# Bias product as a 129th column, chunk rows written by ScalarE, own banks for the last row: a two-layer graph network on one core

## The chip, the cores and the metric

One core of one Trainium2 chip runs the whole kernel. The metric is the device time of one execution in microseconds (us). Five engines work side by side, each in its own program order, and meet only at semaphores: TensorE (PE in the profile), VectorE (DVE), ScalarE (ACT), GpSimd (POOL) and SyncE (SP, which here only issues transfers).

## The reference

Inputs are `x` (4096 x 128), a sparse row-normalised `adj` (4096 x 4096), and small weights. Cut to what matters:

```python
h = relu(layernorm(x))
# first layer: hyperbolic graph layer
g    = h_add(exp0(log0(h) @ embed), embed_bias)
neigh= exp0(adj @ log0(g))
out  = exp0(log0(concat(h, neigh)) @ layer)      # layer = (256 x 128)
x    = x + h_add(out, layer_bias)
h = relu(layernorm(x))
# two attention layers, each:
s = beta * (h/|h|) @ (h/|h|).T ; s = where(adj > 0, s, -1e9)
h = leaky(softmax(s) @ h)                        # slope 0.3
x = x + h
```

Here `exp0(v) = tanh(|v|) v/|v|`, `log0(y) = atanh(|y|) y/|y|`, and `h_add(a, y)` is a weighted sum of `a` and `y` whose two weights need `a.a`, `y.y` and the product `a.y` of each row with the bias `y`.

## The kernel before

Rows are cut in 8 chunks of 512 (4 blocks of 128). Four stages follow one another.

**Opening.** VectorE computes the layer norm, `log0` and the first `h_add`, TensorE the `embed` product and the product of `h` with the upper half of `layer` (`h1_sb`), ScalarE copies them out of PSUM.

**Chunks.** `aggregate` on TensorE multiplies the adjacency tiles of chunk c (loaded by SP in a ring) with all rows: 32 fp32 matmuls of 512 columns. ScalarE copies the result (`at_sb`); after the first tile of the next chunk TensorE runs `layer_product`: four transposes (`rows_ps`) and four matmuls with the lower half of `layer` (`w_ps`). ScalarE takes the squared lengths of the rows (`row_lengths`, L802), and then VectorE runs the chain of the chunk (`gnn_chunk`), a row of dependent instructions on 4 or 8 values per partition (`norm`, `inv_sqrt`, `atanh_over`, `product_scalars`, about 0.2 us each) with passes over 512 columns between them: `t1 = w * scale + h1` (L1283), its squares (L1288), its product with the bias `lb` (L1293), `t2 = lb * weight` (L1305), `t1 = t1 * weight + t2` (L1308), `t1 += x` (L1311), statistics, deviations, `t2` = the normalised rows after relu (L1331), their high and low fp16 halves in `src[0]` (L1334, L1336), and `t3`, the rows of unit length (L1342). ScalarE gives tanh and ln on request (`ask` / `answered`; the counter `asked` goes up on VectorE, `told` on ScalarE), and copies `t1` back to `x_sb`. TensorE transposes `t3` one chunk later (L456, before tile 4 of the chunk after next), ScalarE and VectorE leave it in halves in `xt[0]` (`split_columns`).

**The last chunk beside the first attention slots.** The attention layers work on 72 pairs of chunks (a, b >= a) each in two halves, 144 half-pairs in all, one per slot n of an order written out by hand: scores (`pair_scores`, L622), exp on ScalarE into `values` (`raise_scores`, L990), high halves (`high_halves`, L1000), low halves on VectorE (`low_halves`, L1647), eight transposes for the mirrored block (`turns`, L608), the mask by the adjacency (`own_mask` L1655, `mirrored_mask` L1665), and the weighted sums (`own_sum`, `mirrored_sum`). Slots 0 to 13 don't need chunk 7. So the last chunk's chain (`last_chunk` on VectorE and on ScalarE) is cut in 13 pieces, and `pause(i)` puts slot i + 1 between them. `chunk_norms` comes after pause 2, `chunk_deviations` before pause 9.

**Rows.** Each chunk row a gathers its sums in `own_ps` (two PSUM banks), the mirrored part in `mirror_sums`. At the end of a row VectorE adds both in `sums_in` and inverts the denominators (`row_total`), ScalarE scales (`row_averages`, L1020), VectorE applies leaky and, in the second layer, adds to `x_sb` (`row_leaky`, L1690, L1694). GpSimd stores the chunk (L403). The next row's `own_sum` waits until `own_ps` has been read (`total_made`).

## Time and profile before

| | |
|---|---|
| times of 3 runs | 981.88, 978.26, 982.6 us; median 981.88 |
| profiled execution | 978.14 us, its span 976.6 us, granted TensorE clock 0.989 |
| TensorE matmul busy | 929.2 us, 95% of the span |
| VectorE busy | 818.8 us, 84% |
| ScalarE busy | 511.2 us, 52% |
| GpSimd busy | 8.0 us |
| transfers | 207.26 MB, mean 212 GB/s |

The span runs from the first to the last instruction of one profiled execution; its device time is 1.5 us longer. Busy time of matmuls is modelled, since they are pipelined, so that a share near 100% says that TensorE has no gap, not that it is at its peak. The aggregation runs from about 57 to 291 us, the first attention layer until about 620 us, the rest is the second.

### The profile page before, as it was taken

How to read it: one execution, taken by the hardware profiler on the slowest of the kernel's cores; microseconds unless marked ns; L12 is line 12 of the kernel's file. 1: busy time of each engine (PE TensorE's matmuls, PEld its weight loads, DVE VectorE, ACT ScalarE, POOL GpSimd, SP SyncE). 2: the span in 40 equal slices, each digit the busy share in tenths (PEclk: the TensorE clock that was granted, in tenths of full speed). 3: DMA queues.
4: the chain of work that ended last, by engine and by line, in shares of the span. 5: the costliest groups of instructions: out<-in, count | busy, mean ns of one | idle time of the engine just before them, and what ended most of it. 6: DMA issues, size and time to landing. Idle time of an engine off the chain costs nothing.

```text
span 976.6 us, 22955 instructions
## 1 busy us (share of the span) xinstructions
PE 929.2 (95%) x9012; PEld 695.3 (71%) x9012; DVE 818.8 (84%) x2110; ACT 511.2 (52%) x756; POOL 8.0 (1%) x21
## 2 busy tenths in 40 slices
PE   2989999999996999999999999999999999999996
PEld 2944444444444878888888888778888888888885
DVE  7891888888889987888989898998778887888887
ACT  1711122212126685766656667787565565656564
POOL 0000000000000000000000000000000000000000
PEclk9899999999998999999999999999999999999999
DMA  8338988888861445565465555545565655665630
GB/s 301 143 118 285 307 285 287 277 295 283 301 229 44 174 173 207 196 246 212 179 235 192 222 217 193 180 167 217 197 217 198 246 197 204 221 232 189 246 142 36
DMA packets 29971, 207.26 MB, mean 212 GB/s; under 512 B 3632, under 2 KB 4272, under 8 KB 5296
## 3 DMA queue, kind: packets, MB, share of 16 engines
q1 hardware_dynamic: 28224, 203.44, 57.6%
q0 software_dynamic: 640, 2.10, 0.5%
q8 instruction: 71, 1.16, 0.5%
q10 hardware_dynamic: 1008, 0.33, 0.1%
q14 instruction: 28, 0.23, 0.1%
HBM read 203.75 MB, written 2.10 MB: 211 GB/s over the span
## 4 chain that ended last, share of the span: by engine, by line
PE 69%; DVE 22%; issue 5%; ACT 3%; DMA 1%; DVEq 0%; POOL 0%; SPq 0%; POOLq 0%
PE s_ps L622 17%; PE s_ps L608 10%; PE acc_ps L469 6%; PE acc_ps L675 6%; PE acc_ps L671 6%; PE acc_ps L673 6%; PE acc_ps L652 5%; PE acc_ps L648 5%; PE acc_ps L650 5%; DVE small L1132 1%; DVE small L1134 1%; DVE small L1133 1%; DVE work L1647 1%; ACT work L990 1%; PE s_ps L427 1%
## 5 line engine op out<-in xcount | busy, mean ns | idle before, releaser
L990 ACT ACTIVATE work<-s_ps,beta_bias,beta_scale 128x1024 f32<-128x1024 f32 x144 | 173.4, 1204 | 217.0 <-PE s_ps L622 216.9
L469 PE MATMUL acc_ps<-ring,set 128*128 128x512 f32 x512 | 223.8, 596 | 3.2 <-DVE set L1245 3.2
L1665 DVE SCALAR_TENSOR_TENSOR h_all<-ring,s_ps 128x1024 f32<-128x1024 f32 x112 | 136.7, 1221 | 65.5 <-PE s_ps L608 64.3
L469 PEld LDWEIGHTS acc_ps<-ring,set 128*128 128x128 f32 x512 | 96.8, 191 | 120.3 <-issue 117.6
L1647 DVE TENSOR_TENSOR work<-work 128x1024 f16<-128x1024 f32 x96 | 132.5, 1380 | 5.4 <-ACT work L1000 5.4
L1000 ACT ACTIVATE work<-work 128x1024 f16<-128x1024 f32 x96 | 131.5, 1369 | 3.2 <-DVE work L1655 0.2
L1655 DVE SCALAR_TENSOR_TENSOR work<-ring,work 128x1024 f32<-128x1024 f32 x96 | 116.8, 1217 | 0.0
L622 PE MATMUL s_ps<-xt 128*128 128x512 f16 x432 | 106.4, 382 | 3.8 <-ACT work L990 3.0
L622 PE MATMUL s_ps<-set 128*128 128x512 f16 x432 | 105.0, 379 | 0.5 <-ACT work L990 0.5
L671 PE MATMUL acc_ps<-set,work 128*128 128x129 f16 x576 | 102.4, 219 | 2.7 <-DVE accs L1682 2.7
L671 PE MATMUL acc_ps<-src,work 128*128 128x129 f16 x576 | 103.5, 220 | 1.4 <-DVE work L1655 1.4
L675 PE MATMUL acc_ps<-src,work 128*128 128x129 f16 x576 | 103.9, 224 | 0.0
L673 PE MATMUL acc_ps<-src,work 128*128 128x128 f16 x576 | 103.6, 221 | 0.0
L675 PE MATMUL acc_ps<-set,work 128*128 128x129 f16 x576 | 102.7, 222 | 0.0
L673 PE MATMUL acc_ps<-set,work 128*128 128x128 f16 x576 | 102.5, 219 | 0.0
L652 PE MATMUL acc_ps<-set,h_all 128*128 128x129 f16 x448 | 79.8, 222 | 0.0
L652 PE MATMUL acc_ps<-src,h_all 128*128 128x129 f16 x448 | 79.8, 222 | 0.0
L650 PE MATMUL acc_ps<-src,h_all 128*128 128x128 f16 x448 | 79.6, 219 | 0.0
L650 PE MATMUL acc_ps<-set,h_all 128*128 128x128 f16 x448 | 79.6, 219 | 0.0
L648 PE MATMUL acc_ps<-src,h_all 128*128 128x129 f16 x448 | 79.6, 219 | 0.0
L648 PE MATMUL acc_ps<-set,h_all 128*128 128x129 f16 x448 | 79.6, 219 | 0.0
L608 PE MATMUL s_ps<-ident,work 128*128 128x128 f32 x560 | 73.6, 274 | 3.0 <-DVE work L1647 3.0
(260 smaller groups left out, 1723.2 us busy)
## 6 DMA issues: line engine op xcount, KB each, us to landing
ring<-in_adj_t SPq DMA_DIRECT2D x192, 1024.0 KB, 5.0
x_sb<-in_x SPq DMA_DIRECT2D x4, 512.0 KB, 7.2
out<-x_sb POOLq DMA_DIRECT2D x8, 256.0 KB, 2.8
w<-in_layer ACTq DMA_DIRECT2D x2, 64.0 KB, 8.1
w<-in_embed ACTq DMA_DIRECT2D x1, 64.0 KB, 4.2
eb<-in_embed_bias ACTq DMA_DIRECT2D x1, 64.0 KB, 6.9
lb<-in_layer_bias ACTq DMA_DIRECT2D x1, 64.0 KB, 7.9
beta<-in_beta ACTq DMA_DIRECT2D x2, 0.5 KB, 7.2
```

Source lines behind the costliest of these rows:

```text
L469: last = nc.tensor.matmul(agg, v_sb[:, jb, :], ring[:, k, b, :], start=jb == 0, stop=jb == NB - 1)
L608: ins = nc.tensor.transpose(turn_ps[:, ib, ts(u, P)], words[x.n % WR][:, ds(u * CH + ib * P, P)], ident[:, :])
L622: last = nc.tensor.matmul(score_ps[:, ts(u, CH)], xt[x.la][:, p, ds(x.b * CH + (x.h * HB + u) * P, P)], xt[x.la][:, q, ds(x.a * CH, CH)], ...
L648: nc.tensor.matmul(mir_ps[:, x.h, o], w[:, WORD_HI, col], src[x.la][:, q, F:AW], start=ib == 0, stop=False)
L650: nc.tensor.matmul(mir_ps[:, x.h, ds(u * PW, F)], w[:, WORD_HI, col], src[x.la][:, q, 0:F], start=False, stop=False)
L652: last = nc.tensor.matmul(mir_ps[:, x.h, o], w[:, WORD_LO, col], src[x.la][:, q, F:AW], start=False, stop=ib == CB - 1)
L671: nc.tensor.matmul(own_ps[:, ib // 2, ds(ib % 2 * PW, PW)], w[:, WORD_HI, col], src[x.la][:, q, F:AW], start=opens, stop=False, skip_group ...
L673: nc.tensor.matmul(own_ps[:, ib // 2, ds(ib % 2 * PW, F)], w[:, WORD_HI, col], src[x.la][:, q, 0:F], start=False, stop=False, skip_group_c ...
L675: last = nc.tensor.matmul(own_ps[:, ib // 2, ds(ib % 2 * PW, PW)], w[:, WORD_LO, col], src[x.la][:, q, F:AW], start=False, stop=False, ski ...
L990: nc.scalar.activation(values[x.n % VR], score_ps, ACT.Exp, bias=beta_bias[:, x.la:x.la + 1], scale=beta_scale[:, x.la:x.la + 1]).then_inc ...
L1647: V.tensor_tensor(w[:, WORD_LO, :], values[x.n % VR], w[:, WORD_HI, :], ALU.subtract)\
L1665: V.scalar_tensor_tensor(turned[x.off % MR].rearrange("p (b j) -> p b j", b=CB), ring[:, x.mir_tile % AR, :, ds(x.h * HB * P, HB * P)], 0. ...
```

## The change

The bias product becomes a 129th column of the two products with `layer`: a column `layer @ layer_bias` is appended to `w1` and `w2` (two more VectorE instructions in the opening, for which the first of these products now waits), so `w_ps` and `h1_sb` carry 129 columns, and `t1 . lb` is `bias_column * scale + h1_sb[..., F]`. In the last steps `x` is added while scaling. The high halves of `src[0]` and the unit rows `t3` are made by ScalarE in `rows_out(c)`, which runs behind the copy of chunk c + 1's aggregate; the low halves (`low_part(c)`) are made by VectorE in chunk c + 1 while it waits for tanh. The scores' exp of slot 0 stays ahead of the last chunk's row lengths, its high halves go behind `rows_out`. Pauses 2 and 9 go into the middle of an `inv_sqrt`. The last row of the second layer has its own PSUM banks and its own place for the sums, its division is put behind leaky on VectorE, and its store is issued by SP.

```diff
+        wide_ps = [s_ps[:, i, :].rearrange("p (k n) -> p k n", k=2)[:, :, 0:2 * PW] for i in range(2)]
+        h1_ps = wide_ps + [acc_ps[:, 2:4, 0:2 * PW]]
+        last_own_ps = s_ps[:, 1, :].rearrange("p (k n) -> p k n", k=2)[:, :, 0:2 * PW]
+        sums_last = src0_all[:, 0:2 * CB * PW].bitcast(f32).rearrange("p (b w) -> p b w", w=PW)
...
+            sp.wait_ge(out_ready, NC)
+            sp.dma_start(out_v[:, ds((NC - 1) * CB, CB), :], x_sb[:, ds((NC - 1) * CB, CB), :])\
+                .then_inc(last_stored, 16)
...
-            pe.wait_ge(weights_in, 16 * 5)
+            pe.wait_ge(web_made, 5)
-                if x.n == r.first:
+                if x.n == r.first and x.row != LAST_ROW:
                     wait(pe, total_made, x.row)
+                own_ps = own_of(x.row)
...
+            def rows_out(c):
+                act.wait_ge(asked, (c + 1) * ASKS_CHUNK + start)
+                nc.scalar.activation(src[0][:, ds(c * CB, CB), F:2 * F], t2[:, :, :], ACT.Copy, scale=FS)\
+                    .then_inc(told, 1)
+                act.wait_ge(scaled, c + 1)
+                for b in range(CB):
+                    last = nc.scalar.activation(t3[:, b, :], t2[:, b, :], ACT.Copy, scale=chunk_scale[:, b:b + 1])
+                last.then_inc(xn_ready[0], 1)
                 nc.scalar.activation(at_sb, acc_ps[:, parity, :], ACT.Copy).then_inc(at_ready, 1)
-                row_lengths(c, rows_last_ps if c_last(c) else rows_ps)
+                if not first:
+                    rows_out(c - 1)
+                row_lengths(c)
...
-                pause(-1)
-                row_lengths(c, rows_last_ps)
+                raise_scores(at(0))
+                row_lengths(c)
+                rows_out(c - 1)
+                high_halves(at(0))
                 pause(0)
...
+            for i, (w, column) in enumerate(((w1[:, F:2 * F], w1[:, 2 * F:2 * F + 1]), (w2[:, 0:F], w2[:, F:PW]))):
+                dve.wait_ge(web_made, i + 3)
+                V.scalar_tensor_tensor(bsq[:, :], w, 1.0, lb[:, :], ALU.mult, ALU.mult,
+                                       accum_out=column).then_inc(web_made, 1)
...
-                norm(sm(4, CB), sm(1, CB), lengths, EPS, CB)
-                ask(V.tensor_copy(sm(4, CB), sm(4, CB)))
+                norm(sm(4, CB), sm(1, CB), lengths, EPS, CB, ask)
+                if not first:
+                    dve.wait_ge(told, answers[0])
+                    low_part(c - 1)
+                V.tensor_tensor(in_pairs(sm(9, CB)), bias_column(w_in), in_pairs(sm(3, CB)), ALU.mult)
...
-                for b in range(CB):
-                    ins = V.scalar_tensor_tensor(t2[:, b, :], t1[:, b, :], 1.0, lb[:, :], ALU.mult, ALU.mult,
-                                                 accum_out=small[:, 9, b:b + 1])
+                V.tensor_tensor(sm(9, CB), sm(9, CB), h1_sb[:, rows, F], ALU.add)
+                if not first:
+                    dve.wait_ge(xn_ready[0], c)
...
-                    ins = V.tensor_scalar(t2[:, b, :], lb[:, :], small[:, 13, b:b + 1], None, ALU.mult)
+                    ins = V.scalar_tensor_tensor(t1[:, b, :], t1[:, b, :], small[:, 12, b:b + 1],
+                                                 x_sb[:, c * CB + b, :], ALU.mult, ALU.add)
-                    ins = V.scalar_tensor_tensor(t1[:, b, :], t1[:, b, :], small[:, 12, b:b + 1], t2[:, b, :],
+                    ins = V.scalar_tensor_tensor(t1[:, b, :], lb[:, :], small[:, 13, b:b + 1], t1[:, b, :],
-                ask(V.tensor_tensor(t1[:, :, :], x_sb[:, rows, :], t1[:, :, :], ALU.add))
...
-                step(V.tensor_scalar(src[0][:, rows, F:2 * F], t2[:, :, :], FS, None, ALU.mult))
                 answered()
-                step(V.scalar_tensor_tensor(src[0][:, rows, 0:F], t2[:, :, :], FS, src[0][:, rows, F:2 * F],
-                                            ALU.mult, ALU.subtract))
+                ask(ins)
...
-                for b in range(CB):
-                    ins = V.tensor_scalar(t3[:, b, :], t2[:, b, :], small[:, 1, b:b + 1], FS, ALU.mult, ALU.mult)
-                ins.then_inc(xn_ready[0], 1)
+                V.tensor_scalar(chunk_scale, sm(1, CB), FS, None, ALU.mult).then_inc(scaled, 1)
...
-                for n in range(PAUSES + 1, NH + 5):
+                for n in range(PAUSES + 1, NH + 1):
                     slot(n)
+                own_mask(at(NH - 1))
+                row_total(LAST_ROW - 1)
+                flush(at(NH - 3))
+                row_total(LAST_ROW)
+                row_leaky(LAST_ROW - 1)
+                last_row()
```

## Rows read from the trace of the kernel before

**Rows 1.** Page, part 5, two ScalarE groups of the pairs: x count, busy us, mean ns, idle.

```profile
L990 ACT ACTIVATE work<-s_ps,beta_bias,beta_scale 128x1024 f32<-128x1024 f32 x144 | 173.4, 1204 | 217.0 <-PE s_ps L622 216.9
...
L1000 ACT ACTIVATE work<-work 128x1024 f16<-128x1024 f32 x96 | 131.5, 1369 | 3.2 <-DVE work L1655 0.2
```

**Rows 2.** Windows: busy us of PE, PEld, DVE, ACT, POOL; then clock, DMA share, GB/s.

```profile
295.00:325.00 30.00, 20.63 (x197) 15.42 (x197) 27.48 (x92) 18.83 (x33) 0.00 (x0) 0.89 0.14 45
325.00:356.00 31.00, 28.57 (x365) 24.14 (x363) 29.23 (x68) 18.99 (x29) 0.00 (x0) 1.00 0.51 196
356.00:620.00 264.00, 263.96 (x3278) 221.69 (x3275) 228.57 (x275) 177.88 (x226) 0.24 (x1) 1.00 0.57 210
```

**Rows 3.** Timeline of ScalarE: start us, us, engine, line, what [idle before].

```profile
232.60 0.60 ACT L813 ACTIVATE accs<-acc_ps 128x512 f32<-128x512 f32 x1 [1.79 <-PE acc_ps L469]
...
261.84 0.60 ACT L813 ACTIVATE accs<-acc_ps 128x512 f32<-128x512 f32 x1 [1.57 <-PE acc_ps L469]
266.60 0.28 ACT L802 ACTIVATE accs<-s_ps 128x128 f32<-128x128 f32 x1 [4.17 <-PE s_ps L450]
...
267.53 0.22 ACT L802 ACTIVATION_READ_ACCUMULATOR accs<-s_ps 128x1 f32 x1
...
294.83 0.25 ACT L802 ACTIVATE accs<-acc_ps 128x128 f32<-128x128 f32 x1
```

**Rows 4.** Timeline of VectorE over one chunk of the loop.

```profile
239.53 0.16 DVE L1139 TENSOR_SCALAR small<-small 128x4 f32<-128x4 f32 x1
...
245.53 0.29 DVE L1293 SCALAR_TENSOR_TENSOR t<-t,lb 128x128 f32<-128x128 f32 x1
...
246.50 0.17 DVE L1296 COPY small<-small 128x4 f32<-128x4 f32 x1
...
256.62 0.88 DVE L1305 TENSOR_SCALAR t<-lb,small 128x128 f32<-128x128 f32 x4
257.53 1.14 DVE L1308 SCALAR_TENSOR_TENSOR t<-t,small 128x128 f32<-128x128 f32 x4
...
259.53 0.87 DVE L1314 BATCH_NORM_STATS2 stats<-t 128x6 f32<-128x128 f32 x4
...
266.14 0.16 DVE L1333 TENSOR_TENSOR small<-small 128x4 f32<-128x4 f32 x1
...
268.20 0.87 DVE L1342 TENSOR_SCALAR t<-t,small 128x128 f32<-128x128 f32 x4
268.99 0.16 DVE L1139 TENSOR_SCALAR small<-small 128x4 f32<-128x4 f32 x1
```

**Rows 5.** Timeline of ScalarE, rows of the last chunk scaled.

```profile
357.42 1.28 ACT L854 ACTIVATE t<-t,small 128x128 f32<-128x128 f32 x4
```

**Rows 6.** Timeline of VectorE from the last chunk's start.

```profile
298.58 0.17 DVE L1139 TENSOR_SCALAR small<-small 128x4 f32<-128x4 f32 x1
...
313.93 1.22 DVE L1665 SCALAR_TENSOR_TENSOR h_all<-ring,s_ps 128x1024 f32<-128x1024 f32 x1
...
346.31 0.17 DVE L1393 TENSOR_SCALAR small<-small 128x8 f32<-128x8 f32 x1 [0.66 <-ACT t L842]
...
349.87 1.29 DVE L1647 TENSOR_TENSOR work<-work 128x1024 f16<-128x1024 f32 x1
```

**Rows 7.** Timeline of VectorE in the opening.

```profile
40.01 0.19 DVE L1157 TENSOR_TENSOR small<-small 128x32 f32<-128x32 f32 x1 [1.36 <-ACT small L754]
```

**Rows 8.** Waits of the last 22 us: who <- whom: us, times, longest.

```profile
PE acc_ps L671 <- DVE accs L1682: 1.5, 1, 1.5
```

**Rows 9.** Timeline of VectorE, last row.

```profile
968.51 0.70 DVE L1682 TENSOR_TENSOR accs<-acc_ps,ring 128x516 f32<-128x516 f32 x1 [0.35 <-PE acc_ps L682]
...
971.49 0.69 DVE L1694 TENSOR_TENSOR x_sb<-x_sb,h_all 128x512 f32<-128x512 f32 x1
```

**Rows 10.** Timeline of ScalarE, last row.

```profile
969.46 1.28 ACT L1020 ACTIVATE h_all<-accs,fin 128x128 f32<-128x128 f32 x4 [2.74 <-DVE fin L1685]
```

**Rows 11.** Timeline of GpSimd, last store's issue.

```profile
972.90 0.75 POOL L403 DMA_DIRECT2D out<-x_sb  x1 [3.27 <-DVE x_sb L1694]
```

More of the change, by code:

```diff
@@ L143, in build @@
         lengths = small[:, 11, NB // 2:NB // 2 + CB]
+        chunk_scale = small[:, 9, NB // 2:NB // 2 + CB]
         hh = sb("hh", [P, NB])
@@ L204, in build @@
         lengths_made = sem("lengths_made")
+        scaled = sem("scaled")
         xn_ready = [sem(f"xn_ready{i}") for i in range(2)]
@@ L449, in layer_product @@
                 for b in range(CB):
-                    last = nc.tensor.matmul(w_ps[:, b, :], at_sb[:, ts(b, P)], w2[:, :], start=True, stop=True)
+                    last = nc.tensor.matmul(part(w_ps, b, PW), at_sb[:, ts(b, P)], w2[:, :], start=True, stop=True)
                 last.then_inc(w_done, 1)
@@ L861, in turn @@
                 gnn_chunk(c, parity, first)
-                assert asks[1] == ASKS_CHUNK
+                assert asks[1] == ASKS_CHUNK - 1
             def last_chunk(pause):
@@ L970, in shifted_attention @@
                     turn(NC - 1, 1, False)
+                    rows_out(NC - 1)
                     column_sums_leave(0, 0, early_ps)
@@ L1076, in slot @@
                     high_halves(at(n))
-                if i is not None:
+                if i is not None and i != LAST_ROW:
                     row_averages(i)
@@ L1125, in total, with inv_sqrt @@
                 step(V.tensor_reduce(dst, s, axis=AX.X, op=ALU.add))
-            def inv_sqrt(y, v, t):
+            def inv_sqrt(y, v, t, meanwhile=None):
                 step(V.tensor_scalar(y.bitcast(i32), v.bitcast(i32), 1, None, ALU.logical_shift_right))
                 step(V.tensor_scalar(y.bitcast(i32), y.bitcast(i32), -1.0, float(0x5F3759DF), ALU.mult, ALU.add))
-                for _ in range(3):
+                for i in range(3):
+                    if meanwhile and i == 1:
+                        meanwhile()
                     step(V.tensor_tensor(t, y, y, ALU.mult))
@@ L1265, in split_columns, with in_pairs, low_part @@
                     .then_inc(xt_lo[la], 1)
+            def in_pairs(t):
+                return t.rearrange("p (k b) -> p k b", k=2)
+            def low_part(c):
+                rows = ds(c * CB, CB)
+                V.scalar_tensor_tensor(src[0][:, rows, 0:F], t2[:, :, :], FS, src[0][:, rows, F:2 * F],
+                                       ALU.mult, ALU.subtract)
             def gnn_chunk(c, first):
@@ L1429, in last_chunk @@
                 dve.wait_ge(lengths_made, c + 1)
-                norm(sm(4, CB), sm(1, CB), lengths, EPS, CB)
-                ask(V.tensor_copy(sm(4, CB), sm(4, CB)))
+                norm(sm(4, CB), sm(1, CB), lengths, EPS, CB, ask)
+                dve.wait_ge(told, answers[0])
+                low_part(c - 1)
                 pause(0)
@@ L1625, in shifted_attention @@
                     gnn_turn(NC - 1, False)
+                    dve.wait_ge(told, asks_gnn)
+                    low_part(NC - 1)
                     split_columns(0, NC - 1, slot_ps)
@@ L1677, in row_total @@
                 r = rows_of[i]
-                both = sums_in.rearrange("p (k b) w -> p k (b w)", k=2)
+                sums = sums_last if i == LAST_ROW else sums_in
+                both = sums.rearrange("p (k b) w -> p k (b w)", k=2)
                 if r.a:
@@ L1681, in row_total, with last_row @@
                     dve.wait_ge(flushed, half[r.first].la * NP + r.a * NC - r.a * (r.a + 1) // 2)
-                    V.tensor_tensor(both, own_ps, mirror_sums[:, ds(r.a * CB, CB), :]
+                    V.tensor_tensor(both, last_own_ps if i == LAST_ROW else own_ps, mirror_sums[:, ds(r.a * CB, CB), :]
                                     .rearrange("p (k b) w -> p k (b w)", k=2), ALU.add).then_inc(total_made, 1)
                 dve.wait_ge(total_made, i + 1)
-                V.reciprocal(fin[:, i % 2, 0, :], sums_in[:, :, F]).then_inc(inverse_made, 1)
+                V.reciprocal(fin[:, i % 2, 0, :], sums[:, :, F]).then_inc(inverse_made, 1)
+            def last_row():
+                t, q = rows_x[LAST_ROW % 2], (NC - 1) * CB
+                sums = sums_last[:, :, 0:F]
+                V.scalar_tensor_tensor(t, sums, LEAK, sums, ALU.mult, ALU.max).then_inc(leaked, 1)
+                dve.wait_ge(leaked, LAST_ROW + 1)
+                dve.wait_ge(inverse_made, LAST_ROW + 1)
+                for b in range(CB):
+                    last = V.scalar_tensor_tensor(x_sb[:, q + b, :], t[:, b, :], fin[:, LAST_ROW % 2, 0, b:b + 1],
+                                                  x_sb[:, q + b, :], ALU.mult, ALU.add)
+                last.then_inc(out_ready, 1)
             def row_leaky(i):
```

109 lines of the change are left out of this document (56 added, 53 removed).

## The prediction

> **What bounds the kernel now.** I read the windows first. From 356 us on, where the pairs run alone, TensorE is busy 263.96 of 264 us: nothing is to be had there on another engine. Its gaps lie in the changeover from the aggregation to the pairs: 30.00 - 20.63 = 9.4 us idle at 295 to 325 us and 31.00 - 28.57 = 2.4 us at 325 to 356, while VectorE is busy 27.48 and 29.23 us of these [rows 2]. So VectorE, which runs the last chunk's chain and the first slots by turns, bounds that stretch; the granted clock falls there too (0.89 in the first window, 1.00 in the others).
>
> Then the loop before it. ScalarE's copy of an aggregate starts at 232.60 and 261.84 us: TensorE takes 29.24 us for a chunk. VectorE's chain starts at 239.53 and again at 268.99: 29.46 us. It never waits, and loses 29.46 - 29.24 = 0.22 us a chunk. The row lengths of the chunk that it takes up at 268.99 were made at 267.53 + 0.22 = 267.75 [rows 3, 4], so its arrears are 1.2 us by then, and they end in the changeover. TensorE waits for none of this in the loop.
>
> Last the end: TensorE waits 1.5 us until the row before the last is out of its banks [rows 8], then come total, ScalarE's scaling, leaky, add and store one behind another [rows 9 to 11].
>
> **The loop, VectorE's chain.** From rows 4, start to start:
> - bias product gone: 246.50 - 245.53 = -0.97;
> - L1305, L1308, L1311 took 259.53 - 256.62 = 2.91; now two groups of four of L1308's kind, each 1.14 and 0.09 for the wait behind it: 2.46, so -0.45;
> - behind L1333's start to the next chunk: 268.99 - 266.14 = 2.85. Left are L1333, three small steps of 0.2 (they are in these 2.85) and the new scale, 0.2: 0.97 in all, so -1.88;
> - the copy ahead of tanh goes (-0.20), `low_part` (0.7, L1336 moved) stands in a wait of about 0.3 for tanh: +0.19 for both; two small instructions for the 129th column: +0.24.
>
> 29.46 - 0.97 - 0.45 - 1.88 + 0.19 + 0.24 = 26.6 us. VectorE is then ahead of TensorE. But a second ring forms, through ScalarE: `rows_out(c - 1)` stands ahead of `row_lengths(c)`. From chain start to the finished relu it was 266.14 - 239.53 = 26.61 (L1333 starts right behind it); with 0.19 + 0.24 - 0.97 - 0.45 from above and L1333 put ahead (0.14) it is 25.8. The scale comes 0.85 later, then ScalarE's four copies 1.28 [rows 5], the lengths 267.75 - 266.60 = 1.15 [rows 3], hand-overs 0.1: 29.1 us. That is below TensorE's 29.24 by only 0.1. I take it that the lengths stay where TensorE puts them, so the chunk at 268.99 starts at 267.8: -1.2. If the ring is 0.3 longer than I have it, this 1.2 is not gained.
>
> Queues behind the new waits: ScalarE waits in `rows_out` with the lengths and tanh of the next chunk behind it; TensorE needs the transposes' `t3` half a chunk later, over 10 us of slack. The products in 129 columns instead of 128 I cost at nothing: 8 instructions a chunk, under 1% of 1.1 us.
>
> **The opening.** Two more instructions on VectorE, with their waits 0.65 us, ahead of a wait of 1.36 us for ScalarE [rows 7], which hides them. Uncovered they cost 0.65. The same wait covers that `h1` has three buffers.
>
> **The changeover.** Before, the last chunk's chain starts on VectorE at 298.58 [rows 6]. Now chunk 6 runs from 267.8 for 26.6: free at 294.4. It needs the last row lengths, which ScalarE starts not at 294.83 but before the high halves of slot 0, whose group has a mean of 1.37 [rows 1, 3]: from 293.7 (when the product is there) to 294.85. Start at 294.9: -3.7 us. ScalarE becomes dense here: lengths, `rows_out(6)` 0.6 + 1.28 to 296.6, high halves of slot 0, exp 1.2 and high halves of slot 1, and only then tanh at about 300.4. VectorE, with `low_part(6)` and the low halves of slot 0, asks for it from 299.7 on and waits 0.85. Up to the first mirrored mask, before at 313.93 [rows 6]: -3.7 + 0.75 (`low_part`) + 0.85 (tanh) + 0.24 - 0.97 - 0.20 = -3.0. That mask runs at about 310.9.
>
> From there the slots move together. Sum and statistics save 0.45. The wait of 0.66 for ScalarE's relu stays [rows 6], since the scores that stand ahead of relu move by about 2.8. Pause 9 ahead of six of the nine steps of `inv_sqrt` brings the low halves at 349.87 forward by 1.2: -2.8 - 1.2 = -4.0 there, but the six steps come due in the next slot, where TensorE finds them: -3.4. After that TensorE is the bound, and -3.4 us goes through. TensorE has the gaps for it: 9.4 + 2.4 [rows 2]. Both ends: +1 (the arrears stay, ScalarE's density costs 2 us more than I have) and -7 (three fifths of the 11.8 close).
>
> The clock: 0.89 granted over 30 us is 6.6 us at 1.2 in place of 2.4 GHz (0.22 x 30 at half, the rest at full), behind TensorE's gaps; at most half of it, 3.3 us, is TensorE time lost. The gaps get shorter by my sum, but stay; VectorE bounds there. I count no gain, 0 to 3.3 as bounds, which the -7 takes in.
>
> **The end.** The last row's sums no longer wait for `total_made`: the wait of 1.5 goes, the mask that they need is next, so about -1.2. The total, before at 968.51, starts at 967.3. From then: total and inverse 0.88, the row before's leaky and add 1.44 (they stood ahead of the total before, and are now behind it), leaky 0.72, four scaled adds 1.2: 4.24, done 971.5. Before: 971.49 + 0.69 = 972.18 [rows 9], with ScalarE's 1.28 [rows 10] in it. So -0.65. The store: GpSimd starts its issue at 972.90, 0.72 after, and takes 0.75 [rows 11]. SP's issue of a store is not in the trace. Bounds 0 and -1.47; I take -0.7, the midpoint. The Trainium skill ("DMA: Bandwidth & Descriptors", head table) gives the first byte about 1 us by the GpSimd path and 0.6 us by SP's; by it this term would be -0.4. No row here has a store by SP. End: -1.35, between +0.5 and -2.7.
>
> **Sum.** -3.4 - 1.35 = -4.75 us. The profiled execution took 978.14 us (span 976.6 and 1.5 around it): 973.4. The runs shown are 981.88, 978.26 and 982.6, and against their median 981.88 the sum is 977.1. Two of these four executions lie near 978 and two near 982, so I put the median after between, nearer the upper: 976.0 us.
>
> **Rivals.**
> - *ScalarE takes VectorE's place.* Its list between 291 and 300 us is full, and the ring of 29.1 has 0.1 of room. For it: both numbers. Against: it idles 11 of the 30 us [rows 2]. Then the start gains 2 instead of 3.7, tanh costs 1 more: changeover -0.7, with the end -2: 976.1 by the profiled execution, 979.5 by the median.
> - *More of TensorE's gaps close.* The clock stays at 2.4 GHz, relu isn't waited for. Changeover -6.5, end -2: -8.5: 969.6 and 973.4. Against it: slots from 320 us on have TensorE nearly full, so early work of VectorE finds no gap.
> - *Slower: the ring through ScalarE is the loop's bound.* If `rows_out` adds more than `row_lengths` can bear, arrears grow each chunk. They were 1.2 after six chunks; to eat the 3.4 and lose 5 more needs (8.4 + 1.2) / 6 = 1.6 us a chunk, a ring of 30.8 instead of 29.1. One more load of ScalarE's tables per chunk would do it; the functions are the same ones in the same order, copies and squares ran between tanh and ln before. It decides from a ring of 29.24 on. At 30.8: about 983 by the profiled execution, 987 by the median. That the 129 columns cost the products a second pass would be slower too, but by under 0.1 us each.
>
> **How the numbers follow.** A measurement of this kernel can tell 0.5%, 4.9 us, from no change. Forecast 0.48, first rival 0.27, second 0.18, slower rival 0.07. The forecast's -4.75 lies just inside 0.5%, with a spread of 1.5: its chance of being beyond is 0.5 x 0.48 = 0.24, with the second rival's 0.18 and a little of the first's by chance of the runs: 0.44 faster. Slower by over 0.5%: the third rival's, 0.06. The rest, 0.50, is no change. Range: from the second rival's 969.6 to 973.4, 971.0; to the first's 979.5 and a run more at the upper level, 981.0.
>
> **What would show it.** In the profile after: VectorE waits in the loop for the lengths, about 2.5 us a chunk (right) or never (the chain is not shorter); ScalarE's lengths start right behind the product (right) or behind `rows_out` (the ring). Last chunk's chain at 294.9; first mirrored mask at about 311; TensorE's idle from 295 to 356 about 8.4 instead of 11.8 us. At the end no wait of TensorE between the last two rows, last add done about 4 us after the last total, store issued by SP within 1 us. Wrong, if the aggregation's period is above 29.3 us, or if slots after 356 us take more than before.

## The result, and the profile after

| | before | changed |
|---|---|---|
| median of 15 runs each, taken together | 981.38 us (977.52 to 982.60) | 973.02 us (971.98 to 976.66) |
| mean of these runs | 980.0 us | 973.6 us |
| profiled execution, and its span | 978.14, 976.6 us | 973.76, 972.6 us |

The ratio is 0.9934, 95% interval [0.9920, 0.9948]: 0.66% faster, where I had given faster by over 0.5% a chance of 0.44 and no change 0.50. The forecast was 976.0 us, in a range of 971.0 to 981.0. A second profile of the changed kernel, taken later with 11 runs (median 972.55, mean 973.6), has a span of 971.2 us; I call it the second profile after. The median of before moves more than that of the changed kernel: on other occasions it was 978.49 (29 runs), 979.6 (24) and 978.65 (27). Medians that stand beside each other differ by 8.4 and by 6.1 us, the means by 6.4 and 5.3.

Windows of the changed kernel, columns as in [rows 2], to which the three lines answer (the third ends at 616 instead of 620 us):

```profile
295.00:325.00 30.00, 23.55 (x236) 17.77 (x237) 25.90 (x70) 21.34 (x30) 0.00 (x0) 0.89 0.29 106
325.00:356.00 31.00, 29.11 (x351) 24.01 (x350) 28.50 (x66) 19.92 (x35) 0.25 (x1) 1.00 0.40 142
356.00:616.00 260.00, 259.96 (x3244) 218.95 (x3242) 225.01 (x271) 173.38 (x214) 0.00 (x0) 1.00 0.57 211
```

TensorE's idle in the changeover fell from 9.4 + 2.4 us to 6.4 + 1.9 (8.3 in all, where I had 8.4), and the bulk behind it is full as before. The clock of the first window is 0.89 in both.

ScalarE's timeline in the loop and at the last chunk, against [rows 3]:

```profile
231.11 0.60 ACT L846 ACTIVATE accs<-acc_ps 128x512 f32<-128x512 f32 x1 [3.41 <-PE acc_ps L485]
...
260.35 0.60 ACT L846 ACTIVATE accs<-acc_ps 128x512 f32<-128x512 f32 x1 [3.42 <-PE acc_ps L485]
262.88 0.64 ACT L832 ACTIVATE src<-t 128x512 f16<-128x512 f32 x1 [1.94 <-DVE t L1387]
263.70 1.28 ACT L836 ACTIVATE t<-t,small 128x128 f32<-128x128 f32 x4 [0.18 <-DVE small L1393]
265.11 0.28 ACT L825 ACTIVATE accs<-s_ps 128x128 f32<-128x128 f32 x1
...
292.21 0.28 ACT L825 ACTIVATE accs<-s_ps 128x128 f32<-128x128 f32 x1
...
298.59 0.18 ACT L776 ACTIVATE small<-small 128x4 f32<-128x4 f32 x1
```

The period is 29.24 us, as before. `rows_out` (L832, L836) ends at 264.98 and the row lengths (L825) start at 265.11: by these rows the ring through ScalarE has 0.13 us of room. It is rather more, 0.23 to 0.28, as `a_bias` below shows, since one group may start before the one ahead of it has ended. VectorE's loop, against [rows 4]:

```profile
253.86 1.14 DVE L1360 SCALAR_TENSOR_TENSOR t<-t,small,x_sb 128x128 f32<-128x128 f32 x4
255.03 1.14 DVE L1364 SCALAR_TENSOR_TENSOR t<-lb,small,t 128x128 f32<-128x128 f32 x4
...
263.50 0.17 DVE L1393 TENSOR_SCALAR small<-small 128x4 f32<-128x4 f32 x1
266.36 0.17 DVE L1179 TENSOR_SCALAR small<-small 128x4 f32<-128x4 f32 x1 [2.69 <-ACT accs L825]
...
269.55 0.69 DVE L1317 SCALAR_TENSOR_TENSOR src<-t,src 128x512 f32 x1 [0.36 <-ACT small L776]
```

The chain waits 2.69 us for the lengths; before it never waited. And the changeover on VectorE, against [rows 6]:

```profile
293.67 0.17 DVE L1179 TENSOR_SCALAR small<-small 128x4 f32<-128x4 f32 x1 [0.76 <-ACT accs L825]
...
309.13 1.22 DVE L1712 SCALAR_TENSOR_TENSOR h_all<-ring,s_ps 128x1024 f32<-128x1024 f32 x1
...
343.69 0.17 DVE L1440 TENSOR_SCALAR small<-small 128x8 f32<-128x8 f32 x1 [1.38 <-ACT t L877]
...
346.05 1.33 DVE L1694 TENSOR_TENSOR work<-work 128x1024 f16<-128x1024 f32 x1
```

The last row on VectorE, then SP's store, against [rows 9 to 11]:

```profile
964.27 0.70 DVE L1730 TENSOR_TENSOR src<-s_ps,ring 128x516 f32<-128x516 f32 x1 [0.70 <-PE s_ps L704]
965.00 0.18 DVE L1733 RECIPROCAL fin<-src 128x4 f32<-128x4 f32 x1
965.10 0.66 DVE L1750 SCALAR_TENSOR_TENSOR t<-t 128x512 f32<-128x512 f32 x1
...
967.12 1.14 DVE L1743 SCALAR_TENSOR_TENSOR x_sb<-h_all,fin,x_sb 128x128 f32<-128x128 f32 x4
```

```profile
968.29 0.41 SPq L381 DMA_DIRECT2D out<-x_sb  x1
```

**Where the time went.** I cut each profiled execution at four points: the first pair scores (the aggregation is over), the first mirrored mask (VectorE's job that ends the starving of TensorE), the scores of slot 12 (the chunk's steps are over), those of slot 143, the last, and the last add. All in us:

| | to first scores | to mask | mask to slot 12 | slot 12 to 143 | to last add | to end |
|---|---|---|---|---|---|---|
| before | 290.88 | 23.05 | 43.13 | 599.61 | 15.51 | 4.42 |
| after | 289.38 | 19.75 | 44.95 | 599.61 | 14.57 | 4.30 |
| second after | 289.56 | 19.77 | 43.09 | 599.58 | 14.62 | 4.60 |

The change shortens the way to the mask by 3.30 us and the last row by 0.9. The 1.5 us at the first scores are mostly chance (see "The opening"). The first profile after gives 1.8 of it back between mask and slot 12; the second doesn't.

### The profile page after: what moved, and what is told of

Its sections match the earlier page's. It is cut to its first block, busy times and chain, and to the rows that moved or that the text cites. A ratio compares the mean times of both kernels' runs of the same rounds, so it can differ in the third digit from the quotient of the medians.

```text
span 972.6 us, 22888 instructions
## 1 busy us (share of the span) xinstructions
PE 927.2 (95%) x9012; PEld 693.5 (71%) x9012; DVE 801.0 (82%) x2025; ACT 522.6 (54%) x787; POOL 7.2 (1%) x20
## 4 chain that ended last, share of the span: by engine, by line
PE 86%; DVE 8%; ACT 3%; issue 2%; DMA 1%; SPq 0%; DVEq 0%
PE acc_ps L485 23%; PE s_ps L639 18%; PE s_ps L625 10%; PE acc_ps L697 6%; PE acc_ps L693 6%; PE acc_ps L695 6%; PE acc_ps L670 5%; PE acc_ps L666 5%; PE acc_ps L668 5%; DVE work L1694 1%; ACT work L1028 1%; DVE xt L1244 1%; DVE work L1702 1%; DVE set L1259 1%; DMA x_sb<-in_x 1%
## 5 line engine op out<-in xcount | busy, mean ns | idle before, releaser
L693 PE MATMUL acc_ps<-set,work 128*128 128x129 f16 x560 | 99.6, 219 | 1.2 <-DVE accs L1730 1.2
L697 PE MATMUL acc_ps<-set,work 128*128 128x129 f16 x560 | 99.9, 222 | 0.0
L695 PE MATMUL acc_ps<-set,work 128*128 128x128 f16 x560 | 99.7, 219 | 0.0
```

The lines of the kernel that those rows point to most:

```text
L693: nc.tensor.matmul(own_ps[:, ib // 2, ds(ib % 2 * PW, PW)], w[:, WORD_HI, col], src[x.la][:, q, F:AW], start=opens, stop=False, skip_group ...
L695: nc.tensor.matmul(own_ps[:, ib // 2, ds(ib % 2 * PW, F)], w[:, WORD_HI, col], src[x.la][:, q, 0:F], start=False, stop=False, skip_group_c ...
L697: last = nc.tensor.matmul(own_ps[:, ib // 2, ds(ib % 2 * PW, PW)], w[:, WORD_LO, col], src[x.la][:, q, F:AW], start=False, stop=False, ski ...
```

## The experiments

### Is it the clock that takes 1.8 us back?

The trace's record of the granted clock has a stretch at half speed (1.2 in place of 2.4 GHz) in the changeover of most executions: 303.8 to 310.6 us before, 305.2 to 312.0 after. Before, it ended 3.3 us ahead of the mask at 313.93, while TensorE was short of work; after, it ran 2.9 us past the mask at 309.13. Two kernels put idle products of TensorE into its gaps there, one on each side; they write where nothing is read. `a_fill` is the changed kernel with 26 of them (the two groups below, and 6 on either side of the transposes of the chunk before the last), `b_fill` the kernel before with 33 (11 and 9 in the places below, 13 ahead of these transposes).

```
+            def keep(k):
+                for _ in range(k):
+                    nc.tensor.matmul(acc_ps[:, 1, 3 * P:4 * P], ident[:, :], ident[:, :], start=True, stop=True)
...
+                    if n == 2:
+                        keep(6)
+                    if n == 3:
+                        keep(8)
```

> The changed kernel with 26 idle products of TensorE (128x128, fp32, into columns of PSUM that nothing reads) put in its gaps between the first four pair scores: 6, 6, 6 and 8. The reference's result is unaffected. Theory A (of the 3.4 us forecast for the changeover 1.5 came, since TensorE's clock now halves at 305 to 312 us, where it has work, while before it halved at 304 to 311, where it mostly waited): no half clock near 305, slots 4 to 9 another 1.5 to 2 us earlier than in the changed kernel's profile. Rival B (ScalarE's list or VectorE's chain sets the pace there at either clock): slots stay, or come up to 1 us later by the fillers that stand in the way.

> The kernel before with the same kind of filler in its gaps, 13, 11 and 9 products. Theory A: before the change VectorE bounded the changeover, so a clock that stays up gives 0 to 0.5 us. If it gives 2 us or more, the clock and not VectorE was the bound there, and the account of the profile before was wrong.

Filled changed kernel: 973.14 us (8 runs), ratio to before 0.9943 [0.9921, 0.9964]; no half clock in the changeover, to the mask 19.83, mask to slot 12 43.06. Filled before: 978.47 us, ratio 1.0003 [0.9987, 1.0018]; to the mask 23.10, but then a half-clock stretch of 3.4 us at 315.8, behind the mask: 44.67. So keeping the clock up doesn't shorten the way to the mask in either (VectorE makes it), and what lies behind the mask is 43.1 at full clock. The second profile after tells the same of the unfilled kernel:

> The changed kernel itself, a second profile of it. My theory says that its 64.7 us from the first pair scores to slot 12 hold 1.8 us of one half-clock stretch that falls there by chance of the execution: where it falls elsewhere the stretch takes 62.9. Rival: the stretch is always there (the fall comes from TensorE's gaps in the changeover, which are at the same place each time), then it is 64.7 again. The time of its runs 973.0 by either.

It was 972.55 us, and the half clock did not come. Windows of this second profile, then of the first:

```profile
295.00:325.00 30.00, 22.66 (x247) 17.33 (x248) 27.63 (x76) 21.60 (x30) 0.00 (x0) 1.00 0.30 106
325.00:356.00 31.00, 29.08 (x369) 24.49 (x368) 28.60 (x61) 21.54 (x36) 0.24 (x1) 1.00 0.44 162
305.00:310.00 5.00, 3.92 (x45) 3.02 (x43) 4.66 (x14) 1.43 (x2) 0.00 (x0) 1.00 0.27 57
310.00:315.00 5.00, 4.45 (x54) 3.56 (x52) 4.69 (x13) 2.36 (x3) 0.00 (x0) 1.00 0.36 152
```

```profile
305.00:310.00 5.00, 4.01 (x20) 2.56 (x18) 4.69 (x13) 0.32 (x1) 0.00 (x0) 0.52 0.27 70
310.00:315.00 5.00, 5.00 (x54) 4.19 (x53) 4.31 (x13) 2.56 (x2) 0.00 (x0) 0.80 0.33 139
```

Read the clock beside PE: at 305 to 310 us TensorE is busy for the same 4 us, with 45 products at 1.00 and with 20 at 0.52. My rival, that the fall is there each time, is out. All fourteen profiles of this study agree: from mask to slot 12 it is 43.06 to 43.15 us where no half clock lies behind the mask (nine profiles, both kernels), 43.90 where 0.6 us of it does, 44.95 where 2.9 does, and 44.67, 44.73 and 45.03 where a whole stretch of 3.4 does.

### Is it `rows_out` on ScalarE, or VectorE's shorter chain?

`a_rows_dve` puts the high part and `t3` back on VectorE, with `low_part`, at the end of each chunk; all else is the changed kernel. (ScalarE's call goes in all three places.)

```
-                    rows_out(c - 1)
...
+                V.tensor_scalar(src[0][:, rows, F:2 * F], t2[:, :, :], FS, None, ALU.mult).then_inc(told, 1)
+                answered()
+                low_part(c)
+                for b in range(CB):
+                    ins = V.tensor_scalar(t3[:, b, :], t2[:, b, :], small[:, 1, b:b + 1], FS, ALU.mult, ALU.mult)
```

> The changed kernel with the high halves and unit rows back on VectorE at the end of each chunk (rows_out and low_part's delay undone), all else as changed. VectorE's chain per chunk then is 28.5 us, still under TensorE's 29.24, so the loop does not notice. Theory A: in the changeover VectorE comes free about 1.2 us later than the lengths of chunk 7 need it, but ScalarE is 1.9 us less busy there, so tanh comes sooner: the time is the same within 0.7 us. Rival B (moving this work to ScalarE is what won the changeover): 1.5 to 2 us slower than the changed kernel.

971.73 us (6 runs), ratio 0.9941 [0.9923, 0.9958]; to the mask 19.46. That is 0.3 us less than with `rows_out` on ScalarE. (Its median is lower than that of the changed kernel by 0.8 to 1.3 us, most of which lies behind the last add: see "The end".) The move is worth nothing: VectorE had the room, since with the bias product and the sum's third group gone its chain fits into 29.24 us with the scaling in it. VectorE's timeline of this kernel, at the same place as that of the changed kernel:

```profile
266.49 0.17 DVE L1175 TENSOR_SCALAR small<-small 128x4 f32<-128x4 f32 x1 [1.23 <-ACT accs L825]
```

It still waits 1.23 us a round, and these lengths hang on TensorE's product alone, not on VectorE, as ScalarE's timeline shows:

```profile
265.24 0.28 ACT L825 ACTIVATE accs<-s_ps 128x128 f32<-128x128 f32 x1 [4.17 <-PE s_ps L466]
```

`a_bias` leaves `rows_out` on ScalarE and gives VectorE the bias product back, in the loop (shown) and in the last chunk, as work whose result nobody uses.

```
+                for b in range(CB):
+                    ins = V.scalar_tensor_tensor(t2[:, b, :], t1[:, b, :], 1.0, lb[:, :], ALU.mult, ALU.mult,
+                                                 accum_out=small[:, 2, CB + b:CB + b + 1])
+                step(ins)
-            STEPS = 76
+            STEPS = 77
```

> The changed kernel with the four bias products of each chunk put back as idle work (same operands; in the loop their sums are overwritten, in the last chunk they go to a place that nobody reads; the output is unchanged). They cost 0.97 us a chunk. My theory: VectorE waits about 2.5 us a chunk in the loop, so there the wait only gets shorter (to about 1.5) and the period stays 29.24; in the changeover VectorE bounds, so the stretch from the first pair scores to slot 12 gets longer by 0.97: 62.9 becomes 63.8 us where no half clock falls in it. But this chunk also asks for the next chunk's scale 0.97 later, and the ring through ScalarE had 0.13 of room: rival, the ring becomes the loop's bound, 29.24 becomes 30.1 us a chunk, and the first pair scores come some 5 us later (295). Time by my theory 973.0 + 1 = 974; by the rival 979.

978.13 us (11 runs), ratio to before 1.0002 [0.9985, 1.0018]: the whole gain is gone. My theory (only the wait gets shorter, 974) fell; the rival's mechanism is the right one, and its time too (979). ScalarE's timeline of this kernel, then VectorE's:

```profile
267.45 0.64 ACT L832 ACTIVATE src<-t 128x512 f16<-128x512 f32 x1 [5.47 <-DVE t L1391]
268.27 1.28 ACT L836 ACTIVATE t<-t,small 128x128 f32<-128x128 f32 x4 [0.18 <-DVE small L1397]
269.45 0.25 ACT L825 ACTIVATE accs<-s_ps 128x128 f32<-128x128 f32 x1
```

```profile
240.74 0.17 DVE L1179 TENSOR_SCALAR small<-small 128x4 f32<-128x4 f32 x1 [2.43 <-ACT accs L825]
...
270.67 0.17 DVE L1179 TENSOR_SCALAR small<-small 128x4 f32<-128x4 f32 x1 [2.43 <-ACT accs L825]
```

The lengths now start right behind `rows_out` (1.18 us behind the start of its four copies, against 1.41 in the changed kernel, which leaves a room of 0.23), and the chain comes round in 270.67 - 240.74 = 29.93 us. Less the 0.97 that was put in, the ring takes 28.96, which is 0.28 under 29.24. It loses 0.69 a chunk against TensorE, and the mask comes 24.72 us behind the first scores instead of 19.77. That 4.95 is about six rounds of 0.69 and the 0.97 of the last chunk. Note how the wait misleads: VectorE idles 2.43 us a round (in the changed kernel 2.69), as if there were room; the wait is itself a part of the ring, VectorE to ScalarE and back. I had priced the arrears at the first scores (295 us). These came at 290.25: TensorE doesn't wait in the loop, and the arrears are paid in the changeover.

Two things were not taken apart. The shorter chain was not tried by itself in the kernel before. And ScalarE's new order at the changeover (last row lengths ahead of the high halves of slot 0) is in every version of the changed kernel. By the rows it is worth at most 1.3 us of the 3.30 by estimate: the high halves take 1.34, and VectorE waits 0.76 us for the lengths even so.

### Do the moved pauses bring anything?

```
-                chunk_norms(c, lambda: pause(2))
+                pause(2)
+                chunk_norms(c, None)
...
-                chunk_deviations(lambda: pause(9))
+                chunk_deviations(None)
+                pause(9)
```

> The changed kernel with two of the last chunk's pauses (the places where VectorE turns from the chunk to a slot) back where they were: ahead of the norms and behind all nine steps of the second inverse root. I took 1.2 us of gain for the low halves of slot 9 and 0 for the end of it, as the six steps come due in the next slot. My theory: the low halves of slot 9 come 1.2 us later against the scores of slot 9, and the stretch from the first pair scores to slot 12 stays within 0.4 us of 62.9 (without half clock in it) or of 64.7 (with). Rival: the moved pauses are what let TensorE catch up; then it is 1 to 2 us longer. Time 973.0 by the first, 974.5 by the second.

974.54 us (11 runs), ratio 0.9952 [0.9935, 0.9968], against 0.9947 [0.9930, 0.9964] for the changed kernel beside it. To the mask 19.80. The low halves of slot 9:

```profile
346.72 1.28 DVE L1696 TENSOR_TENSOR work<-work 128x1024 f16<-128x1024 f32 x1
```

These are 36.16 us behind this kernel's mask (310.56). The same two instructions of the second profile after:

```profile
309.33 1.22 DVE L1712 SCALAR_TENSOR_TENSOR h_all<-ring,s_ps 128x1024 f32<-128x1024 f32 x1
...
344.38 1.32 DVE L1694 TENSOR_TENSOR work<-work 128x1024 f16<-128x1024 f32 x1
```

There it is 35.05, so with the old pauses they come 1.1 later, as I had it. Slot 10's scores come 50.90 us behind the first scores, against 50.96. So the move of pause 9 brings its operation forward and no slot. Its execution has a half clock at 348.5 to 351.9 us, which hides what would come behind slot 10. The medians differ by 2.0 us, with intervals that overlap, and 1.1 of it lies outside the span: the device time is 2.16 to 2.65 us above it in ten of the 11 runs, against 1.22 to 1.37 in the changed kernel's beside it; the spans' medians are 972.1 and 971.2.

### The opening

The aggregation ends 1.5 us earlier than before, which I had put at 0. Windows over its start, before and then after:

```profile
57.00:60.00 3.00, 2.59 (x4) 1.17 (x5) 3.00 (x15) 0.00 (x0) 0.00 (x0) 0.67 0.01 3
60.00:65.00 5.00, 5.00 (x11) 2.17 (x10) 5.00 (x24) 0.00 (x0) 0.00 (x0) 0.85 0.21 41
```

```profile
57.00:60.00 3.00, 3.00 (x14) 1.80 (x13) 3.00 (x15) 0.00 (x0) 0.00 (x0) 1.00 0.01 3
60.00:65.00 5.00, 5.00 (x13) 2.13 (x13) 5.00 (x23) 0.00 (x0) 0.00 (x0) 1.00 0.49 156
```

The aggregation starts at 57.41 and 57.69 us, but before at half clock. TensorE's timeline of both shows what stood ahead, first before:

```profile
51.77 2.40 PE L481 MATMUL acc_ps<-src,ident 128*128 128x128 f32 x20
57.41 4.94 PE L469 MATMUL acc_ps<-ring,set 128*128 128x512 f32 x7 [3.24 <-DVE set L1245]
```

```profile
53.08 2.09 PE L457 MATMUL s_ps<-w,src 128*128 128x129 f32 x8 [3.82 <-ACT set L798]
54.96 2.89 PE L497 MATMUL acc_ps<-src,ident 128*128 128x128 f32 x20
57.69 3.60 PE L485 MATMUL acc_ps<-ring,set 128*128 128x512 f32 x8
```

With three buffers for `h1` the last product waits 3.82 us for ScalarE, and the warm-up products behind it close the gap that lay ahead of the aggregation. Three kernels ask whether that is the cause of the 1.5 us: `b_three`, the kernel before with three buffers (`h1_ps[r % 3]`), `b_warm`, the kernel before with 24 warm-ups, and `a_keep`, which is `a_fill` with 14 products in the opening too (and 8 warm-ups instead of 10).

```
-                wait(pe, h1_copied, r - 3)
+                wait(pe, h1_copied, r - 2)
...
-    WARM = 10
+    WARM = 24
...
+                if r == NC - 1:
+                    for _ in range(14):
+                        nc.tensor.matmul(acc_ps[:, 1, 0:P], ident[:, :], ident[:, :], start=True, stop=True)
```

> The kernel before with one thing of the change: three buffers for the copies of h1 where it had four. Theory A (the 1.5 us by which the aggregation ends earlier after the change come from TensorE's clock at its start, and the clock stays up because the third buffer pushes the last product and the ten warm-up products into the gap ahead of it): first pair scores at 289.4 instead of 290.9 us in the profile, TensorE's gap before the aggregation 0 instead of 3.2 us, no half clock between 57 and 65 us, the rest as before; time 1.5 us less. Rival B (the 1.5 us come from the chunk's chain or from the 129th column): first pair scores stay at 290.9 and the time does not move.

> The kernel before with 24 warm-up products ahead of the aggregation where it had 10, four buffers as before. At 0.24 us each (10 took 2.4) they reach from 51.8 to about 57.5 us and close the gap of 3.2. Theory A (clock): aggregation ends 1.5 to 1.7 us earlier (less 0.1 for the start), time 1.5 us less, and runs at the upper level of before (981.5) become rarer. Rival C (it is the buffers themselves, by the order of ScalarE's copies, not TensorE's gap): nothing moves.

> The changed kernel with the fillers of the changeover and 14 more in the 3.8 us gap ahead of the last h1 product in the opening, 8 warm-up products for 10. Theory A: the profile has no half clock between 50 and 70 us nor at 305; beyond the other filler kernel it gains 0 in an execution like the profiled one and up to 3.4 us in those whose half clock fell on the aggregation's start, so the upper levels (973.5, 976.5) become rarer; median about 970. Rival: the levels of the runs have another cause (transfers), and their spread stays.

`b_three`: 977.62 us, ratio 0.9992 [0.9974, 1.0010], first scores at 290.35. `b_warm`: 976.99, ratio 0.9992 [0.9979, 1.0006], 289.41. `a_keep`: 972.91 (6 runs), ratio 0.9933 [0.9908, 0.9958], 289.30. In the medians there is nothing that can be told, and `a_keep` missed its 970: its runs have a mean granted clock of 0.996 to 0.998 and still lie between 970.85 and 974.02, as its rival had it.

The profiles tell more if the aggregation's start is kept apart from its length (first product to first scores). The length is 231.70 to 231.77 us in the ten profiles without half clock in it, `b_three` among them, and 233.18 to 233.71 in the four with it: before, `b_tail`, `b_fill` and `b_warm`. So `b_three` bears theory A out in its one profile (the buffers move the half clock ahead of the aggregation, which is worth about 1.8 us), and `b_warm` does not: its half clock lies at 56.3 to 59.8 us, and its early first scores come from an early start.

The start is another matter. TensorE's first products of the opening take nearly twice their later time, though the record of the granted clock says 1.00 there, and how long they do so differs between executions. Timeline of TensorE, before and then after:

```profile
24.93 1.91 PE L427 MATMUL s_ps<-w,src 128*128 128x128 f32 x8
28.25 1.06 PE L427 MATMUL s_ps<-w,src 128*128 128x128 f32 x8
```

```profile
20.69 1.67 PE L443 MATMUL s_ps<-w,src 128*128 128x128 f32 x8
23.48 1.06 PE L443 MATMUL s_ps<-w,src 128*128 128x128 f32 x8
```

Sorted by the number of such slow groups of eight, the fourteen profiles give (us):

| slow groups | aggregation starts, four buffers | first scores | starts, three buffers | first scores |
|---|---|---|---|---|
| 1 | 55.89, 55.95 | 289.60, 289.41 | 57.69 to 58.10 (5 profiles) | 289.38 to 289.80 |
| 2 | 57.41 (before) | 290.88 | 58.55, 58.65, 59.06 | 290.25, 290.35, 290.76 |
| 3 | 59.63 | 292.82 | | |

`a_keep` (two) and `a_best` (three) have fillers in the opening and start at 57.53 and 59.41. So three buffers start the aggregation 1.1 to 2.2 us later, and the half clock that they keep out of it gives 1.5 to 2.0 back: in like executions the first scores come 0.1 to 0.6 us earlier with two slow groups, and with one between 0.2 us earlier and 0.4 later. The 1.50 between the two profiles is for the most part chance, since before had two slow groups and the changed kernel one. What sets their number isn't shown.

### The end

`b_tail` is the kernel before with the last row's part of the change alone (banks of its own, the order behind the last slot, SP's store); `a_pool` is the changed kernel with the last store issued by GpSimd again, which is the diff shown; the lines of `b_tail` are those of the change.

```
-            sp.wait_ge(out_ready, NC)
-            sp.dma_start(out_v[:, ds((NC - 1) * CB, CB), :], x_sb[:, ds((NC - 1) * CB, CB), :])\
-                .then_inc(last_stored, 16)
-            sp.wait_ge(last_stored, 16)
...
-            with pool.Fori(0, NC - 1) as c:
+            with pool.Fori(0, NC) as c:
```

> The kernel before with the last row's part of the change alone: own banks, division behind leaky on VectorE, store by SP. The tail is apart from all else: 1.05 us less, as between the two profiles (972.6 - 968.6 against 976.6 - 971.6 from the last scores on). A rival would be that the tail gains only with the earlier work of the rest: 0.

> The changed kernel with the last store issued by GpSimd as before. In the two profiles GpSimd's issue started 0.72 us after the last add and took 0.75, SP's started 0.03 after it and took 0.41. Theory A: 0.7 to 1.1 us slower than the changed kernel at the end. Rival B: the landing hides the issue, under 0.2.

`b_tail`: 976.74 us, ratio 0.9983 [0.9967, 1.0000]. `a_pool`: 974.05 us, ratio 0.9961 [0.9944, 0.9977]. From the last scores to the last add it is 15.51 us in the kernel before and 14.56 to 14.62 in every kernel with the new last row: -0.94. From there to the end of the span it is 4.38 to 4.42 in the four profiles with the old end. With SP's store it is 3.01 to 3.25 in five of nine, and 4.30 to 4.60 in the other four, both profiles of the changed kernel among them; `a_pool` has 5.08. GpSimd's issue in `a_pool` begins 0.71 us behind the last add, SP's in the changed kernel 0.03:

```profile
967.54 0.75 POOL L415 DMA_DIRECT2D out<-x_sb  x1 [1.03 <-DVE x_sb L1739]
```

In three of the long ones (`after_again`, `a_fill`, `a_keep`) the store's data are not what is late. In the second profile after they have landed at 969.35 us and all other engines' closing instruction is at 969.75, but VectorE's at 971.22. In the first profile after it is both: the store lands 3.47 us behind the last add where it is 2.50 to 2.84 in the other eight, and VectorE closes 0.4 us behind the rest. What holds VectorE I don't know.

It goes with the kernel and not with the execution, as far as the runs can tell. The device time is 1.15 to 1.37 us above the span in every run of the changed kernel, `a_fill` and `a_keep` (40 runs), and 1.44 us or more in every run of all others. From the last add to the end of the device time it is 5.92 to 5.96 us in the four profiles with the old end, 4.55 to 4.69 in `b_tail`, `a_rows_dve`, `a_bias` and `a_best`, but 5.50 and 5.93 in the changed kernel's two, 5.71 to 5.87 in `a_fill`, `a_keep` and `a_pauses`, and 6.63 in `a_pool`. So SP's store brings 1.3 us in four kernels and 0 to 0.5 in the changed one, and between kernels with different ends up to 1.4 us of a difference of medians lies here. Against `a_pool` the changed kernel's end is 0.7 to 1.1 us shorter, as theory A had it; the medians (974.05 against 972.55 to 973.14) have the same sign, with intervals that overlap.

### A version of both

From the above: `rows_out` on VectorE, and the opening's fillers of `a_keep` (none in the changeover).

> The changed kernel with the scaling of the rows (high part and t3) back on VectorE, and in the opening 8 warm-up products instead of 10 and 14 idle products ahead of the last h1 product, so that TensorE enters the aggregation at full clock. If both count, 971.7 (as the first alone) or a little below, first scores at 289.3, stretch to slot 12 62.6 us. If the opening's products only move the half clock to a later place, it may fall into the changeover, and the time is 973 or more. That ScalarE's rows_out brings something in the medians (rival): 973 to 974.

970.40 us (5 runs), ratio to before 0.9911 [0.9888, 0.9934]; the changed kernel beside it 972.55 and 0.9947 [0.9930, 0.9964]. It has the lowest median of the study, 2.1 us under the changed kernel's and 1.3 under that of `a_rows_dve`; the intervals overlap. Of the 2.1, 1.2 us are the shorter end (4.69 against 5.93 us behind the last add), so what the two edits themselves bring isn't shown. Its profiled execution (973.43) was the slowest of its five, with three slow groups in the opening and a half clock until 311.3, 0.6 us past the mask.

## Why the prediction was right, point by point

- **The loop.** Chain 26.6 us: measured 263.67 - (266.36 - 29.24) = 26.55. Ring through ScalarE 29.1: by `a_bias` 29.93 - 0.97 = 28.96, by the changed kernel's rows 29.24 - 0.23 = 29.0. Chunk taken up 1.2 us earlier: against the first scores 1.13. That TensorE's period stays: yes. The slower rival, a ring beyond 29.24, was described rightly, and `a_bias` shows how near it was: 0.97 us more in VectorE's chain is enough for it. I had priced it for an excess of 1.6 us a chunk (983 and 987 us, which leave out my own -1.35 at the end; with it they are 981.8 and 985.5); at 0.69 it takes back the gain and no more.
- **The changeover, to the mask.** VectorE free 294.4 - 290.88 = 3.5 us behind the first scores: measured 3.53. Chain's start 4.0: 4.29. Wait for tanh 0.85: 0.29, so that the mask came 3.30 us earlier, not 3.0.
- **Behind the mask.** I had -3.4 in the end, from -4.0 at the low halves of slot 9. These came 4.2 earlier (346.05 has the clock in it, so by the second profile: 344.38 - 289.56 = 54.8 for 59.0), and slot 12 3.3 earlier. The number holds, though my step from -3.0 at the mask to -2.8 behind it had no term. Of my two reasons one doesn't: the moved pause adds nothing, and neither does the sum's 0.45, since from mask to slot 12 it is 43.1 us in both kernels. What counts is the mask alone. VectorE's wait for ScalarE's relu was to stay 0.66 and became 1.38 in both profiles, at no cost.
- **The clock.** I counted no gain, with 0 to 3.3 as bounds. The half clock cost nothing before, as it lay in time in which TensorE waited for VectorE. With the mask 3.3 us earlier a stretch at nearly the same place reaches into work, and the first profile pays 1.8: a loss, a sign that my bounds left out. Against it stand profiles without any half clock in the changeover: the second profile after, `a_pool` and `a_rows_dve`. Of the unfilled kernels with before's changeover all four profiles have it. So the second rival (more gaps closed, the clock stays) is right in part; with so few profiles its share can't be told.
- **The end.** The total 1.2 earlier: 1.26 (10.58 us behind the last scores, before 11.84). Total to last add 4.24: measured 968.26 - 964.27 = 3.99; so the part -0.65 is -0.94. Store -0.7: its issue ends 0.44 us after the last add instead of 1.47, -1.03, and the span's end comes 1.1 to 1.4 us earlier or hardly moves (-0.1 to +0.2), by a wait that I didn't know of. In the first profile it is -0.12. The Trainium skill ("DMA: Bandwidth & Descriptors", Specifications) gives the first byte about 1 us by GpSimd's path and 0.6 us by SP's, an estimate of 0.4 us for the difference. No row here shows a first byte; from the issue's start to the landing the store takes 2.53 to 2.56 us by GpSimd in four profiles (3.24 in `a_pool`) and 2.47 to 2.81 by SP in eight (3.44 in the first profile after), so in the whole way no such difference is seen. What the rows show is that the issue itself begins 0.7 us earlier on SP.
- **The opening.** Put at 0 with a cover of 1.36 us. The cover is there only in some executions: with one slow group VectorE has no wait at that place, before or after, and its first piece for the aggregation comes 0.5 to 0.8 us later (55.99 to 56.22 us against 55.40 and 55.45), which is my 0.65 uncovered. That the buffers are covered was wrong: the last product waits 3.82 us, and the aggregation starts 1.1 to 2.2 us later. What I did not see either is that this moves the warm-up up to the aggregation and the half clock out of it, which gives as much back.
- **The sum.** -4.75 against 978.14: 973.4, measured 973.76. By parts of the span: opening -1.50, mask -3.30, clock +1.82, last row -0.94, store -0.12, that is -4.04. That the number is so near is luck in part: two terms that I had at 0 cancel within 0.3, and both are chance of the two executions (two slow groups against one in the opening, the place of the half clock). The second profile has -5.4. What the change brings in both profiles is the mask's 3.30 and the last row's 0.94, 4.24 in all, and up to 0.5 at the end. The means differ by 5.3 to 6.4; the rest, about 1 us, I can't place. The 976.0 that I gave was higher by the 2.6 us that I added for before's upper level; the changed kernel's own runs lie near 972 and 974, with three of 15 at 976.5. The first rival (ScalarE takes VectorE's place) did not come about.

## What to carry to other kernels

Where an engine waits in every round and is still on a ring of two engines, its wait is no room: add up the ring (chain, hand-over, the other engine's work until it hands back) and compare it with the round of the bounding engine; here 2.7 us of wait stood for less than 0.3 us of slack, and 0.97 us of extra work lost all 5 us. Arrears of a loop whose bound does not wait show only where the next stage begins, so multiply the excess of a round by the rounds. Moving work to the idler engine is worth nothing if the round fits without the move: try the shorter chain alone first. And compare stages between profiles only where the stages ahead went alike: here 1.5 us at the first scores were mostly the luck of the opening, and up to 1.4 us of a difference of medians lay behind the last add.

## What the runs showed of the hardware

- The place of TensorE's half-clock stretches differs between executions of one kernel (first two profiles of the changed kernel: 305.2 to 312.0 us, and none between 57 and 965), and it costs by what lies in it: 0 where TensorE is waiting anyway, 1.5 to 1.9 us for 3.4 us in full work.
- Idle products in the changeover left both kernels' medians where they were (973.14 against 973.02 and 972.55 for the changed one, where the clock stayed at 1.00; 978.47 against 979.6 for before, where the half clock came later, at 315.8 us).
- The opening's products took nearly twice their later time until about 23, 28 or 32 us, by the execution, while the granted clock was recorded as 1.00; the aggregation's start moved with it, 55.9, 57.4 and 59.6 us in the kernels with four buffers.
- The closing instruction of VectorE is 0.4 to 1.6 us behind all others in four of nine profiles with SP's store, those of the changed kernel, `a_fill` and `a_keep`, with the store's data landed; this hides the faster issue.
